# Up projection of a product-key layer in three fp32r passes, and its GpSimd sums in sixteen pieces

## The reference, cut to what matters

```
q = (x @ Wq).reshape(b, t, H, 2, DK)                 # H = 4 heads, two halves of 64
sim1, sim2 = q1 . keys[:, :, 0], q2 . keys[:, :, 1]  # 128 keys each
s1, i1 = top_k(sim1, 8); s2, i2 = top_k(sim2, 8)
all_scores = s1[..., :, None] + s2[..., None, :]     # 64 candidates
final_scores, pk_idx = top_k(all_scores, 8)
final_indices = i1 * 128 + i2 of those
hidden = silu(x . e_down[final_indices]) * relu(final_scores)
out = sum(hidden * e_up[final_indices])              # e_down, e_up: 2048 x 256
```

## Time and profile before

| | |
|---|---|
| median of 3 runs | 4386.55 us (4381.77 to 4388.78) |
| the profiled execution, its own time | 4390.64 us |
| its span (first to last instruction) | 4388.9 us |
| mean granted TensorE clock | 0.943 |
| PE busy | 3856.2 us, 88% of the span |
| DVE busy | 2624.5 us, 60% |
| ACT busy | 1997.4 us, 46% |
| POOL busy | 901.4 us, 21% |

### The profile page before, as it was taken

One profiled execution on the slowest core, in us unless ns is written; L12 is line 12 of the kernel. 1 busy time (PEld: TensorE's weight loads), 2 busy tenths in 40 slices (PEclk: granted clock), 3 DMA queues, 4 the chain that ended last, 5 costly groups with the idle time before them and its releaser, 6 DMA issues. The chain is left out here.

```text
span 4388.9 us, 76482 instructions
## 1 busy us (share of the span) xinstructions
PE 3856.2 (88%) x26248; PEld 3265.7 (74%) x26248; DVE 2624.5 (60%) x6005; ACT 1997.4 (46%) x5211; POOL 901.4 (21%) x743
## 2 busy tenths in 40 slices
PE   6776999999898876999999999799989998887791
PEld 5555888889776765788888888688878886666671
DVE  7887999999576336555555555444433334666533
ACT  6885666666323433444434443333333333775140
POOL 1113323233001331000000000122223332001245
PEclk9997999999998997999999999899999998998695
DMA  2001000000001013111111111422232221002244
GB/s 71 18 12 46 1 0 0 0 0 1 27 22 46 0 51 140 46 40 40 40 37 35 40 40 39 115 70 68 66 105 73 72 74 43 13 14 67 73 135 130
DMA packets 148634, 209.45 MB, mean 48 GB/s; under 512 B 20576, under 2 KB 87424, under 8 KB 147968
## 3 DMA queue, kind: packets, MB, share of 16 engines
q1 hardware_dynamic: 141488, 187.14, 13.9%
q0 software_dynamic: 6864, 18.75, 1.5%
HBM read 178.18 MB, written 27.66 MB: 47 GB/s over the span
## 5 line engine op out<-in xcount | busy, mean ns | idle before, releaser
L1241 ACT ACTIVATE peer_tab<-peer_sims 128x128 f32<-128x128 f32 x1024 | 305.7, 394 | 0.0
L1248 POOL TENSOR_TENSOR peer_tab<-peer_sims 128x2048 f32<-128x2048 f32 x64 | 247.2, 3882 | 276.8 <-ACT peer_sims L1225 248.4
L1296 DVE SCALAR_TENSOR_TENSOR peer_tab<-peer_tab,peer_th 128x2048 f32<-128x2048 f32 x128 | 298.4, 2374 | 2.6 <-ACT peer_tab L1241 2.3
L1313 PE MATMUL bank<-ident,peer_tab 128*128 128x128 f32 x2048 | 247.8, 275 | 23.7 <-DVE peer_tab L1296 23.7
L1313 PEld LDWEIGHTS bank<-ident,peer_tab 128*128 128x128 f32 x2048 | 234.5, 142 | 37.1 <-DVE peer_tab L1296 24.6
L1363 PE MATMUL bank<-peer_wd,peer_hh 128*128 128x256 f32 x1024 | 246.4, 384 | 2.5 <-DVE peer_hh L1354 2.5
L1336 PE MATMUL bank<-peer_hT,peer_wg 128*128 128x256 f32 x1024 | 244.4, 382 | 0.0
L651 DVE TENSOR_TENSOR moe2a_b<-moe2a_a,moe2a_spread 128x512 f32<-128x512 f32 x104 | 78.4, 754 | 235.9 <-ACT moe2a_a L625 232.7
L1336 PEld LDWEIGHTS bank<-peer_hT,peer_wg 128*128 128x128 f32 x1024 | 196.2, 192 | 26.6
L1363 PEld LDWEIGHTS bank<-peer_wd,peer_hh 128*128 128x128 f32 x1024 | 185.2, 190 | 30.7 <-DVE peer_hh L1354 7.5
L651 DVE TENSOR_TENSOR moe2b_b<-moe2b_a,moe2b_spread 128x512 f32<-128x512 f32 x96 | 68.0, 708 | 233.1 <-ACT moe2b_a L625 232.7
(11 more groups left out here) (503 smaller groups left out, 10996.3 us busy)
## 6 DMA issues: line engine op xcount, KB each, us to landing
mha_wo<-mha_wo SPq DMA_DIRECT2D x128, 256.0 KB, 2.6
moe2b_spread<-moe_shares SPq DMA_DIRECT2D x48, 256.0 KB, 3.1
moe2a_spread<-moe_shares SPq DMA_DIRECT2D x40, 256.0 KB, 3.5
m_y_rows<-moe_y SPq DMA_DIRECT2D x79, 128.0 KB, 1.7
att_ctxT<-in_ctxT_dram SPq DMA_DIRECT2D x32, 256.0 KB, 2.6
lin_ctxT<-in_ctxT_dram SPq DMA_DIRECT2D x16, 256.0 KB, 2.6
mem_ctxT<-in_ctxT_dram SPq DMA_DIRECT2D x16, 256.0 KB, 2.6
mem_ctx<-in_ctx_dram SPq DMA_DIRECT2D x16, 256.0 KB, 2.9
```

The source lines that it names most:

```text
L1241: i = nc.scalar.activation(tab[g][h][:, b * P:(b + 1) * P], sims[:, g, 1, h, :], ACT.Identity, bias=sims[:, g, 0, h, b:b + 1])
L1248: nc.gpsimd.tensor_tensor(out=tab[g][h][:].rearrange("p (a b) -> p a b", b=P), in0=sims[:, g, 1, h, :].unsqueeze(1).broadcast_to([P, NB, P ...
L1296: nc.vector.scalar_tensor_tensor(out=tab[g][h][:], in0=tab[g][h][:], scalar=th[:, g, h:h + 1], in1=tab[g][h][:], op0=ALU.is_ge, op1=ALU.mu ...
L1313: i = nc.tensor.matmul(TB[n % 2][:, j * P:(j + 1) * P], tab[g][h][:, blk * P:(blk + 1) * P], core.ident[:], start=(j == 0 and h == 0), sto ...
```

## The change

The weights `wg` of the up projection and its input `hT` are each kept as two fp32r tensors, a high half and a low half (the rest), and each product of the up projection is the sum of three fp32r matmuls: high x high, high weight x low input, low weight x high input. The halves of `wg` are made once, on the chip: two transfers put the raw weights into two of the score tables that aren't in use yet (group 1, heads 2 and 3), ScalarE copies the high halves and GpSimd subtracts the low halves at p = 2 of tile -1; the first sums of group 1 on both engines and the first up projection wait for that. `hand_over_dve` makes the halves of `hT` with a copy and a subtraction.

To make room, `cwT` becomes five half tables in place of two full ones (group 0's first half single, its second half double, group 1 single), with the waits that go with it, and the columns of `a` and `hh` are ordered by group and block instead of by block. `wd` has a semaphore of its own.

Each of GpSimd's sums becomes sixteen operations of 128 columns with one tensor operand and one scalar per partition. `past` and the weighing become `scalar_tensor_tensor` operations in place of `tensor_scalar` and `tensor_tensor`; `past` gets a constant tile of ones, which GpSimd sets at the start and on which DVE waits once.

```diff
-    wg, wd = sb("wg", [P, C, E]), sb("wd", [P, NB, D])
+    wg, wd = [sb(n, [P, C, E], FP32R) for n in ("wg_hi", "wg_lo")], sb("wd", [P, NB, D])
+    PARTS = ((0, 0), (0, 1), (1, 0))
...
-    hTf, hT = sb("hTf", [P, C, PU]), [sb(f"hT{i}", [P, C, PU]) for i in range(2)]
+    hTf, hT = sb("hTf", [P, C, PU]), [[sb(f"hT_{n}{i}", [P, C, PU], FP32R) for n in ("hi", "lo")] for i in range(2)]
...
-    cwT = sb("cwT", [P, 2, NB, PU])
+    cwT = sb("cwT", [P, 5, NB // 2, P])
...
-        nc.vector.tensor_copy(hT[par][:], hTf[:]).then_inc(hT_ready, 1)
+        nc.vector.tensor_copy(hT[par][0][:], hTf[:]).then_inc(hT_hi_made, 1)
+        dve.wait_ge(hT_hi_made, t + 1)
+        nc.vector.scalar_tensor_tensor(out=hT[par][1][:], in0=hTf[:], scalar=1.0, in1=hT[par][0][:],
+                                       op0=ALU.mult, op1=ALU.subtract).then_inc(hT_ready, 1)
...
     def sums_act(act, t, g, h):
         sims_wait(act, t, g)
         sums_free(act, t, g)
+        if is_first(t) and g == 1:
+            act.wait_ge(wg_lo_made, C)
...
     def sums_pool(pool, t, g, h):
         sims_wait(pool, t, g)
         sums_free(pool, t, g)
-        nc.gpsimd.tensor_tensor(out=tab[g][h][:].rearrange("p (a b) -> p a b", b=P),
-                                in0=sims[:, g, 1, h, :].unsqueeze(1).broadcast_to([P, NB, P]),
-                                in1=sims[:, g, 0, h, 0:NB].unsqueeze(2).broadcast_to([P, NB, P]), op=ALU.add).then_inc(sum_pool, 1)
+        if is_first(t) and g == 1:
+            pool.wait_ge(wg_lo_made, C)
+        pool.sem_inc(passed, 1)
+        for b in range(NB):
+            i = nc.gpsimd.tensor_scalar(tab[g][h][:, b * P:(b + 1) * P], sims[:, g, 1, h, :], sims[:, g, 0, h, b:b + 1], None, ALU.add)
+        i.then_inc(sum_pool, 1)
...
-        nc.vector.tensor_scalar(past[:], i1[:], float(NB), None, ALU.is_ge)
+        nc.vector.scalar_tensor_tensor(out=past[:], in0=i1[:], scalar=float(NB), in1=fixed[:].unsqueeze(1).broadcast_to([P, NH, TOP]),
+                                       op0=ALU.is_ge, op1=ALU.mult)
...
+    def part_of(par, g, half):
+        return 3 + half if g else (1 + par if half else 0)
...
-        if g == 0 and n == 0 and some((t - 1) * SLOTS):
-            act.wait_ge(hh_ready, (t - 1) * SLOTS)
+        used = (t - 1) * SLOTS + 2 * n + 2 if g == 1 or n < 2 else (t - 1) * SLOTS
+        if some(used) and (not isinstance(t, int) or t > 0):
+            act.wait_ge(hh_ready, used)
...
         for n in range(2):
             blk = 2 * p + n
-            for c in range(C):
-                i = nc.tensor.matmul(GB[p % 2][:, n * PU:(n + 1) * PU], wg[:, c, blk * P:(blk + 1) * P], hT[par][:, c, :],
-                                     start=(c == 0), stop=(c == C - 1))
+            for m, (pw, ph) in enumerate(PARTS):
+                for c in range(C):
+                    i = nc.tensor.matmul(G[:, :, n, :], wg[pw][:, c, blk * P:(blk + 1) * P], hT[par][ph][:, c, :],
+                                         start=(m == 0 and c == 0), stop=(m == len(PARTS) - 1 and c == C - 1))
         i.then_inc(g_ready, 1)
...
-        nc.vector.tensor_tensor(out=hh[:, p % 2, :], in0=a[:, p % 2, :],
-                                in1=cwT[:, par, 2 * p:2 * p + 2, :].rearrange("p b t -> p (b t)"), op=ALU.mult).then_inc(hh_ready, 1)
+        first = part_of(par, 0, p // 4)
+        nc.vector.scalar_tensor_tensor(out=hh[:, p % 2, :].rearrange("p (g k) -> p g k", g=PG), in0=a[:, p % 2, :].rearrange("p (g k) -> p g k", g=PG),
+                                       scalar=1.0, in1=cwT[:, first:3 + p // 4 + 1:3 + p // 4 - first, 2 * p % 8:2 * p % 8 + 2, :].rearrange("p g b t -> p g (b t)"),
+                                       op0=ALU.mult, op1=ALU.mult).then_inc(hh_ready, 1)
...
+            if p == 2 and isinstance(t, int) and t == -1:
+                for c in range(C):
+                    split_pool(pool, c)
...
+    raw_wg = [tab[1][2][:], tab[1][3][:]]
+
+    def split_act(act, c):
+        act.wait_ge(tables_in, 16 * C)
+        nc.scalar.activation(wg[0][:, c, :], raw_wg[c], ACT.Copy).then_inc(wg_hi_made, 1)
+
+    def split_pool(pool, c):
+        pool.wait_ge(wg_hi_made, c + 1)
+        nc.gpsimd.tensor_tensor(out=wg[1][:, c, :], in0=raw_wg[c], in1=wg[0][:, c, :], op=ALU.subtract).then_inc(wg_lo_made, 1)
...
-            sp.dma_start(wg[:], args["e_downT"].rearrange("(c p) h -> p c h", p=P)).then_inc(tables_in, 16)
-            sp.dma_start(wd[:], args["e_up"].rearrange("(n p) d -> p n d", p=P)).then_inc(tables_in, 16)
+            for c in range(C):
+                sp.dma_start(raw_wg[c], args["e_downT"][c * P:(c + 1) * P, :]).then_inc(tables_in, 16)
+            sp.dma_start(wd[:], args["e_up"].rearrange("(n p) d -> p n d", p=P)).then_inc(wd_in, 16)
```

More of the change, by code:

```diff
@@ L1105, in peer_stage @@
     i1, past = sb("i1", [P, NH, TOP], U32), sb("past", [P, NH, TOP])
-    rest = sb("rest", [P, PG])
+    rest, fixed = sb("rest", [P, PG]), sb("fixed", [P, TOP])
+    fixed_set = sem("fixed_set")
     tab = [[sb(f"tab{g}{h}", [P, E]) for h in range(NH)] for g in range(PG)]
-    cwT = sb("cwT", [P, 2, NB, PU])
+    cwT = sb("cwT", [P, 5, NB // 2, P])
     a, hh = sb("a", [P, 2, 2 * PU]), sb("hh", [P, 2, 2 * PU])
     GB, TB, IB, YB = bank[0:2], bank[2:4], bank[4:6], bank[6:8]
-    weights_in, tables_in, passed = sem("weights_in"), sem("tables_in"), st.passed()
+    weights_in, tables_in, wd_in, passed = sem("weights_in"), sem("tables_in"), sem("wd_in"), st.passed()
+    wg_hi_made, wg_lo_made, hT_hi_made = sem("wg_hi_made"), sem("wg_lo_made"), sem("hT_hi_made")
     var_ready, rstd_ready, xn_ready, hT_ready = sem("var_ready"), sem("rstd_ready"), sem("xn_ready"), sem("hT_ready")
@@ L1318, in table_act @@
         act.wait_ge(t_filled, t * PG * NTAB + g * NTAB + n + 1)
-        if g == 0 and n == 0 and some((t - 1) * SLOTS):
-            act.wait_ge(hh_ready, (t - 1) * SLOTS)
-        nc.scalar.activation(cwT[:, par, 4 * n:4 * n + 4, g * P:(g + 1) * P], TB[n % 2][:].rearrange("p (b t) -> p b t", t=P),
+        used = (t - 1) * SLOTS + 2 * n + 2 if g == 1 or n < 2 else (t - 1) * SLOTS
+        if some(used) and (not isinstance(t, int) or t > 0):
+            act.wait_ge(hh_ready, used)
+        nc.scalar.activation(cwT[:, part_of(par, g, n // 2), n % 2 * 4:n % 2 * 4 + 4, :], TB[n % 2][:].rearrange("p (b t) -> p b t", t=P),
                              ACT.Copy).then_inc(t_emptied, 1)
@@ L1327, in up_pe @@
         if is_first(t) and p == 0:
-            pe.wait_ge(tables_in, 32)
+            pe.wait_ge(wg_lo_made, C)
+            pe.wait_ge(wd_in, 16)
         if p == 0:
@@ L1332, in up_pe @@
             pe.wait_ge(a_ready, k - 1)
+        G = GB[p % 2][:].rearrange("p (g b t) -> p g b t", g=PG, t=P)
         for n in range(2):
             blk = 2 * p + n
-            for c in range(C):
-                i = nc.tensor.matmul(GB[p % 2][:, n * PU:(n + 1) * PU], wg[:, c, blk * P:(blk + 1) * P], hT[par][:, c, :],
-                                     start=(c == 0), stop=(c == C - 1))
+            for m, (pw, ph) in enumerate(PARTS):
+                for c in range(C):
+                    i = nc.tensor.matmul(G[:, :, n, :], wg[pw][:, c, blk * P:(blk + 1) * P], hT[par][ph][:, c, :],
+                                         start=(m == 0 and c == 0), stop=(m == len(PARTS) - 1 and c == C - 1))
         i.then_inc(g_ready, 1)
@@ L1362, in down_pe @@
             for g in range(PG):
-                i = nc.tensor.matmul(YB[par][:, g * D:(g + 1) * D], hh[:, p % 2, n * PU + g * P:n * PU + (g + 1) * P], wd[:, 2 * p + n, :],
+                i = nc.tensor.matmul(YB[par][:, g * D:(g + 1) * D], hh[:, p % 2, (2 * g + n) * P:(2 * g + n + 1) * P], wd[:, 2 * p + n, :],
                                      start=(p == 0 and n == 0 and g == 0), stop=(p == SLOTS - 1 and n == 1), skip_group_check=True)
@@ L1411, in tile_act @@
                 scores_act(act, t + 1, nxt, 1)
+            if p == 2 and isinstance(t, int) and t == -1:
+                for c in range(C):
+                    split_act(act, c)
             if p >= 4 and exists(t + 1):
@@ L1487, in _ @@
         def _(dve):
+            dve.wait_ge(fixed_set, 1)
             dve.sem_inc(y_used, 1)
@@ L1494, in _ @@
         def _(pool):
+            nc.gpsimd.memset(fixed[:], 1.0).then_inc(fixed_set, 1)
             core.clear_stale(pool)
```

## The result

The change makes the kernel slower: 4583.60 us (median of 4 runs, 4580.92 to 4593.36) against 4384.75 (4 runs of before, 4381.77 to 4388.78), a ratio of 1.0456 with a 95% interval from 1.0441 to 1.0471. The forecast was 4351 and its range ended at 4390. The profiled execution has a span of 4591.6 us, 202.7 more than before.

A forecast was written before the change was run, and what follows sets the result against it. PE was taken to bound the layer at 48.2 us a tile, falling to 46.0 with DVE at 45.6; 35 us saved and 0 for the start gave 4351 against 4386.55, range over all 4336 to 4390.

The forecast's parts named there:

- I take 0.30, the copy of the same shape, the one input streamed; ends 0.22 and 0.41: GpSimd's sums: each new operation of 128 columns takes 0.30 us, between 0.22 and 0.41.
- sum for DVE: DVE's time in a steady tile: own need plus waits for GpSimd, 45.6 us against PE's 46.0, so PE stays the bound.
- rival A: Picks and masks: GpSimd's pieces hold DVE up, 16 waits of 0.30 us in two groups; 4419 us, chance 0.21.
- it waits for DVE too: A GpSimd sum running beside a DVE mask took 5.57 us instead of 3.8, read as GpSimd waiting for DVE.
- PE's sum: Up projection: twelve fp32r matmuls in 1.44 us replace 1.72 us, saving 0.28 us a slot, 35 us over 125 slots.
- rival C: Up projection: an fp32r pass costs as much as an fp32 record, 110 us lost, 4497 us; chance 0.03.
- DVE's own need of 41.2: DVE in a steady tile: 39.8 us without the waits taken out, with the change's additions together 41.2 us.
- The 0.06 for the weighing's new form: DVE's weighing as scalar_tensor_tensor: 0.75 us at 512 columns against 0.69, 8 x 0.06 = 0.5 us a tile.
- DVE's waits for short pieces, 2.2 us a group: DVE waiting for GpSimd's short operations: 1.6 us a group plus 0.6 at the fourth mask, under the 2.4 available.
- The fourth mask: DVE's last mask of a group needs the last GpSimd sum and waits a further 0.6 us for it.
- The start: Splitting wg before group 1's first sums and first table: net effect taken as 0, ends -5 and +9 us.
- what would show it: Signs listed beforehand; wrong if PE idles behind DVE's masks, GpSimd's operations take 0.4, or a fourth mask waits for GpSimd.

The follow-up runs named there:

- experiment 3: The changed kernel with a plain copy of 128 columns in place of each of GpSimd's sixteen additions a sum; 4347.44 us, 0.9902 of before.
- experiment 2: The kernel before with only GpSimd's sums each made as sixteen scalar operations, up projection left in fp32; 4566.59 us, 1.0402 of before.
- experiment 11: The kernel before with only GpSimd's sums each made as four operations of 512 columns, up projection left in fp32; 4382.45 us, 0.9986 of before.

## Why the prediction was wrong

**The step that failed** is "I take 0.30, the copy of the same shape, the one input streamed; ends 0.22 and 0.41" in the sum for DVE. The piece measured 0.602, outside both ends. The ends came from a scalar operation of two columns and a cast from integers. A copy of 128 columns, run in this place, does take 0.293; a scalar operation with the same input costs twice that. The row with the right operation had two columns, the row with the right size was a copy, and neither carries over to the other. The estimate of 0.41 in rival A, from the Trainium skill, "GPSIMD Engine Reference", section 3, was nearer and still too low.

**The sum that was missing** is the second error. Two sums were made, for PE and for DVE. At 0.30 a piece GpSimd has 64 x 0.30 = 19 us of a tile to do, and no third seemed needed. At 0.602 it has 38.5, which alone would still fit into 46.0. But it takes turns with the masks besides, and for that wait no sum had a term, though the prediction had read it in a row ("it waits for DVE too"). In the changed kernel 112 pieces, seven a tile, began inside a mask and took 2.39 to 2.93 us in place of 0.60: in the stretch above that is 13 of the 53.07 - 37.1 = 16.0 us that GpSimd is busy beyond its own time. With the 5.9 us that it idles for the norm this makes up the 59.0.

How often pieces meet a mask hangs on their length: 41 of the copies did so, and 113 pieces of two tensors of 128 columns. So the sum was needed inside the prediction's own ends as well. At 0.398, below the upper end of 0.41, the tile is already 48.3, and GpSimd's stream fills it.

Point by point:

- *PE's sum held.* The timeline after shows twelve matmuls in pairs, 0.238 us from pair to pair, 0.119 a pass:

```profile
705.78 1.89 PE L1384 MATMUL bank<-peer_wd,peer_hh 128*128 128x256 f32 x8
707.32 0.58 PE L1355 MATMUL bank<-peer_hT_hi,peer_wg_hi 128*128 128x256 f32 x2
707.74 0.40 PE L1355 MATMUL bank<-peer_hT_lo,peer_wg_hi 128*128 128x256 f32 x2
707.98 0.40 PE L1355 MATMUL bank<-peer_hT_hi,peer_wg_lo 128*128 128x256 f32 x2
...
708.93 1.91 PE L1328 MATMUL bank<-ident,peer_tab 128*128 128x128 f32 x16
```

  The first pair counts 0.42, so a slot's up projection is 1.61 and not 1.44; but the down projection in front of it is shorter by as much, 1.54 us from start to start. The same down projection in the kernel before (its next start is 654.47):

```profile
652.74 1.89 PE L1363 MATMUL bank<-peer_wd,peer_hh 128*128 128x256 f32 x8
```

  Down and up together take 3.15 us, against 1.73 + 1.72 = 3.45 before: 0.30 saved, forecast 0.28. That the two shifts cancel was not foreseen. The tile of experiment 3, 45.67, is 2.61 under that of before. The weight loads are hidden, as taken: rival C did not happen.
- *DVE's own need of 41.2 was too high.* With memsets, where nothing of GpSimd's is in its way, DVE is busy 319.40 of 400 us, 36.5 a tile. "Smaller waits are left in", said the step; they were several us. The 0.06 for the weighing's new form did not show (686 ns before and after); the low half took 0.693 for 0.75, `past` 0.243 for 0.25.
- *DVE's waits for short pieces, 2.2 us a group, were too high as well.* With copies DVE is busy 324.18 of 400 us against 319.40 with memsets: 0.55 us a tile for the two groups, not 4.4. These two errors lie on the safe side (37.0 of 45.67 us in place of 45.6 of 46.0), which is why the forecast holds once the piece is 0.29.
- *The fourth mask* was to wait 0.6 us for the last sum; it waits 7.46.
- *The start* was put at 0, -5 to +9. With copies it is so: the second hand-over comes at 413.98 against 416.48. With long pieces the split adds to them: the second hand-over is 29.9 us late in the changed kernel, 19.7 with the pieces alone (experiment 2).
- *Rival A* had the side, and the fourth mask named in "what would show it". Its mechanism, sixteen waits of DVE at 0.30 each, is not what happened: DVE waits after issue hardly at all, and its price, 4419, was a sixth of the loss, 32 of 199 us.

The new up projection can be kept: with sums of four operations the tile is 47.34, and the time 0.9977 of before. Of the 40 us that the copies show to be there, about 10 are had, and not all by the new up projection: the four operations alone give 0.9986 (experiment 11), and the two intervals overlap. Against that run the tile is 0.74 us shorter, 10 us in fourteen tiles, but the second hand-over comes 12 us later (424.16 against 411.92), so the start takes it back. Against the copies the fourteen tiles lack 14 x 1.67 = 23 us and the start 10. What would bring these is open; a sum on GpSimd that reads nothing from SBUF was not tried.

## To carry to other kernels

Price a short GpSimd operation by a row of the same kind at the same size; a copy says nothing of a scalar operation, and more operands can be cheaper than fewer. When a change multiplies instructions on an engine that had time to spare, make the sum for that engine too, with what it waits for its neighbour, and say from which length of the piece on it becomes the bound (here somewhere between 0.29 and 0.40 us, 64 pieces in a tile of 46). To ask whether a suspect decides, put something cheaper in its place: the copies gave the forecast's time back in one experiment.

## What the runs showed of the hardware that was not expected

- On GpSimd a scalar operation of 128 columns takes 0.602 us with a scalar per partition and 0.524 with a constant, more than one with two tensors, 0.398. Two-tensor operations with broadcast operands lie on one line: 0.398 at 128, 1.035 at 512 and 3.607 (minimum) at 2048 columns, 1.67 ns a column and 0.18 fixed. Two full tensors cost more: the low halves of `wg`, 2048 columns each with an fp32r output, took 4.50 and 4.54 us.
- GpSimd's pieces wait for a whole mask of DVE (up to 2428 ns for a copy of 0.293), but the masks hardly wait for short pieces: 2.452 us against 2.347. For pieces of 1.035 us DVE's short operations wait: `wc` of 64 columns took up to 1.08 us in place of 0.28.
- Memsets of 128 columns, 0.204 us, run beside DVE's weighings and masks with no wait on either side.
- In front of an fp32r up projection the fp32 down projection takes 1.54 us from start to start in place of 1.73, and the first fp32r pair takes 0.42 in place of 0.24; the two cancel.
- The fp32r matmuls of 256 columns start 0.119 us apart with new weights each time, beside weight loads recorded at 186 ns and more.
